# A macaron block in fp32 products: transposes of both layers moved from TensorE to transposing DMAs of 16-bit halves

## The reference

```
x = x + 0.5 * ffn(layernorm(x))
x = x + attn(layernorm(x))
x = x + 0.5 * ffn(layernorm(x))

ffn(x):  shared = silu(x @ Ws_up) @ Ws_down
         aff = x @ centroids.T;  top 8 of 64 experts by aff + bias
         w = sigmoid(aff of the chosen) / their sum
         routed = sum over the chosen experts of w_e * (silu(x @ W_up[e]) @ W_down[e])
attn(u): xf = u[:1], then u[1:] @ WB.T;  xb = u[1:] @ WBf.T, then u[-1:]
         gamma = sigmoid(xf @ w1 + xb @ w2 + b);  y = gamma * (xf + xb) + (1 - gamma) * u
```

## Time and profile before

| | |
|---|---|
| median of 3 runs | 790.46 us (790.07 to 790.76) |
| the profiled execution, its own time | 790.69 us |
| its span, first to last instruction | 788.5 us |
| PE busy | 777.0 us (99%) |
| DVE busy | 656.8 us (83%) |
| ACT busy | 634.4 us (80%) |
| POOL busy | 436.6 us (55%) |
| granted clock of TensorE | full (2.4 GHz) over all the span |

### The profile page before, as it was taken

The page is one execution under the profiler, slowest core; times in us unless marked ns, Lnnn a source line. Parts: engine busy times, 40 slices in busy tenths (PEclk is TensorE's granted clock), DMA queues, the critical chain, the costliest instruction groups (busy, mean ns, idle before and its releaser), DMA issues.

```text
span 788.5 us, 12421 instructions
## 1 busy us (share of the span) xinstructions
PE 777.0 (99%) x3621; PEld 641.4 (81%) x3621; DVE 656.8 (83%) x1423; ACT 634.4 (80%) x1221; POOL 436.6 (55%) x404
## 2 busy tenths in 40 slices
PE   7999999999999999999999999999999999999998
PEld 6777878888888888888888888888888888888786
DVE  6787989879898798977989789897898888788875
ACT  7987778888878888778887779787788887886885
POOL 4785646565555554645646456464554645554453
PEclk9999999999999999999999999999999999999999
DMA  8000000100000000100001000010000000000000
GB/s 287 15 1 14 1 1 1 27 16 16 11 8 21 27 13 0 27 0 27 13 0 27 0 27 13 0 27 0 27 13 0 13 1 27 13 1 1 13 1 14
DMA packets 26973, 14.66 MB, mean 19 GB/s; under 512 B 13248, under 2 KB 25792, under 8 KB 26944
## 3 DMA queue, kind: packets, MB, share of 16 engines
q1 hardware_dynamic: 26944, 14.30, 6.2%
HBM read 9.05 MB, written 2.10 MB: 14 GB/s over the span
## 4 chain that ended last, share of the span: by engine, by line
PE 86%; DVE 6%; ACT 5%; issue 2%; POOL 1%; ACTq 0%; DVEq 0%
PE up L855 13%; PE up L857 13%; PE up L856 13%; PE y_ps L855 13%; PE y_ps L857 13%; PE y_ps L856 13%; PE side L864 2%; ACT g_hi L520 2%; ACT up L486 2%; PE side L873 2%; DVE gated L709 1%; DVE g_lo L718 1%; PE side L906 1%; PE side L905 1%; POOL g_lo L373 1%
## 5 line engine op out<-in xcount | busy, mean ns | idle before, releaser
L373 POOL TENSOR_TENSOR g_lo<-gated,g_hi 128x512 fp32r<-128x512 f32 x256 | 331.6, 1296 | 309.9 <-ACT g_hi L520 309.4
L486 ACT ACTIVATE up<-up 128x512 f32<-128x512 f32 x513 | 302.2, 589 | 63.5 <-PE up L857 62.4
L709 DVE TENSOR_TENSOR gated<-up,cw 128x512 f32<-128x512 f32 x256 | 175.6, 686 | 73.0 <-ACT up L486 68.4
L855 PE MATMUL y_ps<-g_hi,wd_hi 128*128 128x512 f32 x512 | 204.3, 399 | 1.3 <-POOL g_lo L373 1.2
L855 PE MATMUL up<-x_hi,wu_hi 128*128 128x512 f32 x512 | 200.5, 392 | 1.0 <-DVE g_lo L718 1.0
L857 PE MATMUL y_ps<-g_hi,wd_lo 128*128 128x512 f32 x512 | 199.9, 390 | 0.0
L857 PE MATMUL up<-x_hi,wu_lo 128*128 128x512 f32 x512 | 199.6, 390 | 0.0
L856 PE MATMUL y_ps<-g_lo,wd_hi 128*128 128x512 f32 x512 | 199.5, 390 | 0.0
L856 PE MATMUL up<-x_lo,wu_hi 128*128 128x512 f32 x512 | 199.3, 389 | 0.0
L709 DVE TENSOR_TENSOR up<-up,cw 128x512 f32<-128x512 f32 x256 | 177.0, 691 | 19.7 <-ACT up L486 17.7
L520 ACT CAST g_hi<-up 128x512 fp32r<-128x512 f32 x256 | 151.6, 592 | 46.2 <-DVE up L709 43.7
(11 more groups left out here) (128 smaller groups left out, 518.1 us busy)
## 6 DMA issues: line engine op xcount, KB each, us to landing
x_in<-in_x SPq DMA_DIRECT2D x8, 256.0 KB, 2.7
wu_raw<-in_w_up SPq DMA_DIRECT2D x4, 512.0 KB, 7.9
wd_raw<-in_w_down SPq DMA_DIRECT2D x4, 512.0 KB, 8.6
x_res<-in_x SPq DMA_DIRECT2D x8, 256.0 KB, 2.8
out<-out_sb SPq DMA_DIRECT2D x7, 256.0 KB, 2.2
mix<-in_mix SPq DMA_DIRECT2D x1, 389.0 KB, 7.3
out<-out_sb SPq DMA_DIRECT2D x2, 128.0 KB, 1.9
cw_halves<-w_halves SPq DMA_TRANSPOSE x12, 2.7
```

The source lines that it names most:

```text
L373: nc.gpsimd.tensor_tensor(g_lo[:, i, :], gated[:, t // 2 % ORING, :], g_hi[:, i, :].bitcast(fp32), ALU.subtract).then_inc(lo_done[1], 1)
L486: nc.scalar.activation(up[i][:, :], up[i][:, :], ACT.Silu).then_inc(silu_done, 1)
L709: nc.vector.tensor_tensor(gated[:, t // 2 % ORING, :] if t % 2 else up[i][:, :], up[i][:, :], cw[ph.q][:, :], ALU.mult).then_inc(gate_done, 1)
L855: nc.tensor.matmul(o, a[0], b[0], start=start, stop=False)
```

## The change

In phases 3 to 13 no transposes on PE are left. Each of the five paths (weights, x of the first layer, x of the third layer, u, y) goes this way: the fp32 values are taken as pairs of 16-bit words; POOL copies the first words of all values side by side, then the second words (two packs, `pack`); SP issues one transposing DMA for the 128 x 1024 words; POOL writes the turned halves back into their places (two joins, `join_...`). For y, ACT's copy out of PSUM packs itself, by writing the two kinds of words apart. The weights' join moves from ACT to POOL. The copies on ACT of x and of u go. In phase 2 the new x of the first layer goes by DMA too, with its packs in phase 1, and phase 2 packs the x of the third layer for phase 3. `x1` and `last_sum` read the joined y in SBUF. SP's order becomes, in the loop: x of the third layer, y, load of x, store, load of the residual, weights, x of the first layer, y, u, weights.

The tables move steps to other slots (before and after):

```
 AT_THIRD = {
-    "x_t": 4, "x_copy": 4, "x_split": 5, ... "cw_pack": (15, 17), "cw_copy": 23,
+    "x_join": (1, 3), "x_split": 5, ... "cw_pack": (17, 21), "cw_join": (25, 27),
...
-    "stat2": (29, 30), "aggr2": 30, "rstd2": 31, "norm2": (33, 34),
+    "stat2": (29, 30), "aggr2": 30, "rstd2": 31, "norm2": (33, 34), "x2_pack": (33, 34),
 AT_STEADY_A = {
-    "x_t": 6, "x_copy": 6, "x_split": 9, "aff": 10, "sig": 13, "bias": 11, "max": 13, "take": 13,
-    "gate": 13, "sum": 13, "inv": 21, "cw_pack": (21, 23), "cw_copy": 29,
-    "y_t": 6,
-    "stat0": (20, 22), "aggr0": 24, "rstd0": 25, "norm0": (28, 30),
-    "y": 2, "out": 8, "keep": 11,
+    "x2_join": (1, 3), "x_split": 15, "aff": 9, "sig": 13, "bias": 11, "max": 13, "take": 13,
+    "gate": 13, "sum": 13, "inv": 21, "cw_pack": (21, 23), "cw_join": (29, 31),
+    "y_join": (5, 7), "out": 10, "keep": 13, "y": 2,
+    "stat0": (16, 17), "aggr0": 18, "rstd0": 19, "norm0": (22, 24), "x_pack": (25, 27), "x_join": (33, 34),
 AT_STEADY_B = {
-    "x_t": 1, "x_copy": 1, "x_split": 3, "aff": 6, "sig": 8, "bias": 7, "max": 8, "take": 8,
-    "gate": 8, "sum": 8, "inv": 15, "cw_pack": (15, 17), "cw_copy": 23,
-    "y_t": 6, "x1": 8, "stat1": (10, 12), "aggr1": 13, "rstd1": 14, "norm1": (16, 18), "xu": 19, "u_t": 22,
-    "u_copy": 22, "attn": 25, ...
+    "x_split": 9, "aff": 5, "sig": 8, "bias": 7, "max": 11, "take": 11,
+    "gate": 12, "sum": 12, "inv": 15, "cw_pack": (25, 26), "cw_join": (29, 30),
+    "y_join": (5, 7), "x1": 7, "stat1": (8, 9), "aggr1": 10, "rstd1": 10, "norm1": (13, 14), "xu": 23, "u_pack": (15, 17), "u_join": (19, 21),
+    "attn": 25, ... "norm2": (33, 34), "x2_pack": (33, 34),
```

The new steps:

```
+            def turn(halves, turned, done):
+                rows_in = halves.rearrange("p h n c -> p (h n c)") if len(halves.shape) == 4 else halves.rearrange("p h t -> p (h t)")
+                sp.dma_start(turned[:, :, :, :].rearrange("p h n c -> p (h n) c"), rows_in, transpose=True).then_inc(done, 16)
...
+            def pack(halves, h, made, words_of, value, done):
+                if h == 0:
+                    hold(pool, made, value)
+                last = nc.gpsimd.tensor_copy(halves[:, h, :, :], words_of)
+                if h == 1:
+                    last.then_inc(done, 1)
...
+            def join_x(q, h, moved, value, splits):
+                if h == 0:
+                    hold(pool, x_lo_done[1 - q], splits)
+                    hold(pool, moved, value)
+                made = nc.gpsimd.tensor_copy(words(x_raw[:, :], h), plane(n_turned_halves, h))
...
+            def join_u(c, h):
...
+                made = nc.gpsimd.tensor_copy(words(u_mid[:, 1:T], h), plane(n_turned_halves, h)[:, 1:T])
...
+            def join_y(ph, h):
+                dst = out_sb if ph.post is not None else x1
...
+                made = nc.gpsimd.tensor_copy(blocks_of(dst[:, :, :], h), y_turned_halves[:, h, :, :])
...
-            def cw_join(ph):
-                act.wait_ge(cw_moved, 16 * (ph.p - 1))
-                nc.scalar.copy(halves_of(cw[1 - ph.q][:, :], NB), cw_halves[:, :, :, :]).then_inc(cw_done[1 - ph.q], 1)
...
+                if by_dma:
+                    planes = y_ps[:, :].bitcast(u16).rearrange("p (t h) -> p h t", h=2)
+                    nc.scalar.copy(y_halves, planes).then_inc(y_copied, 1)
...
-                        nc.vector.scalar_tensor_tensor(x1[:, :, :], side_rows[0], 0.5, x_res[:, :, :],
+                        nc.vector.scalar_tensor_tensor(x1[:, :, :], x1[:, :, :] if ph.y_dma else side_rows[0], 0.5, x_res[:, :, :],
```

More of the change, by code:

```diff
@@ L51, in __init__ @@
         self.late_act = at.get("late_act", self.late)
-        self.cw_dma = prep is not None and "cw_pack" in at
+        self.cw_dma, self.x_dma = "cw_pack" in at, prep is not None and "x_t" not in at
+        self.y_dma, self.u_dma = "y_join" in at, "u_join" in at
         self.use = p // 2 if isinstance(p, int) else use
@@ L380, in pack_weights @@
-                halves = w_norm[:, :, :].bitcast(u16).rearrange("p n (e h) -> p n e h", h=2)[:, :, :, h]
-                made = nc.gpsimd.tensor_copy(w_halves[:, :, h, :].rearrange("p n (e r) -> p n e r", r=R),
-                                             halves.unsqueeze(3).to_broadcast([P, NB, E, R]))
+                if h == 0:
+                    hold(pool, dup_done[1 - ph.q], n + 1 - (ph.q == 1))
+                made = nc.gpsimd.tensor_copy(w_halves[:, h, :, :].rearrange("p n (e r) -> p n e r", r=R),
+                                             blocks_of(w_norm[:, :, :], h).unsqueeze(3).to_broadcast([P, NB, E, R]))
@@ L383, in pack_weights, with join_weights @@
                 if h == 1:
                     made.then_inc(w_packed, 1)
+            def join_weights(ph, h):
+                q = 1 - ph.q
+                if h == 0:
+                    hold(pool, cw_moved, 16 * (ph.p - 1))
+                made = nc.gpsimd.tensor_copy(words(cw[q][:, :], h), plane(cw_turned_halves, h))
+                if h == 1:
+                    made.then_inc(cw_done[q], 1)
+            def join_x(q, h, moved, value, splits):
+                if h == 0:
+                    hold(pool, x_lo_done[1 - q], splits)
+                    hold(pool, moved, value)
+                made = nc.gpsimd.tensor_copy(words(x_raw[:, :], h), plane(n_turned_halves, h))
+                if h == 1:
+                    made.then_inc(x_copied[q], 1)
@@ L425, in phase @@
                         pack_weights(ph, ph.at["cw_pack"].index(t))
+                    if t in ph.at.get("cw_join", ()):
+                        join_weights(ph, ph.at["cw_join"].index(t))
+                    if t in ph.at.get("x_pack", ()):
+                        h = ph.at["x_pack"].index(t)
+                        pack(n_halves, h, norm_done[0], blocks_of(normed[0][:, :, :], h), ph.norm0 + 1, x_packed)
+                    if t in ph.at.get("x_join", ()):
+                        c = ph.norm0 if ph.norm0 is not None else ph.prep[2]
+                        join_x(1, ph.at["x_join"].index(t), x_moved, 16 * (c - 1), c)
+                    if t in ph.at.get("x2_join", ()):
+                        join_x(0, ph.at["x2_join"].index(t), x2_moved, 16 * ph.prep[2], ph.prep[0])
+                    if t in ph.at.get("x2_pack", ()):
+                        h = ph.at["x2_pack"].index(t)
+                        pack(n_halves, h, norm_done[2], blocks_of(normed[2][:, :, :], h), ph.mid + 1, x2_packed)
+                    if t in ph.at.get("u_pack", ()):
+                        h = ph.at["u_pack"].index(t)
+                        pack(n_halves, h, norm_done[1], blocks_of(normed[1][:, :, :], h), ph.mid + 1, u_packed)
+                    if t in ph.at.get("u_join", ()):
+                        join_u(ph.mid, ph.at["u_join"].index(t))
+                    if t in ph.at.get("y_join", ()):
+                        join_y(ph, ph.at["y_join"].index(t))
                     if ph.at.get("xu") == t:
@@ L570, in phase @@
                     if ph.at.get("cw_copy") == t:
[L571 to L574, removed]
+                        cw_copy(1 - ph.q, ph.prep[0])
                     if ph.at.get("u_copy") == t:
@@ L989, in phase @@
                     if ph.at.get("y_t") == t:
[L990 to L993, removed]
+                        pe.wait_ge(cw_done[ph.q], ph.use + 1)
                         turn_y(ph.p)
```

82 lines of the change are left out of this document (60 added, 22 removed).

## The result

The changed kernel takes 792.00 us (median of 20 runs, 791.25 to 793.26) against 790.48 us before (20 runs, 790.07 to 791.27). The ratio is 1.0019, with a 95% interval of 1.0013 to 1.0026. The forecast was 785.4 us, faster; 792.00 lies within its range of 779 to 794 us, but on the other side of the kernel before. The transposes left PE as forecast and nothing was gained: the time that they took came back as waits of PE.

What follows compares the result with a forecast made beforehand. PE, busy 99% of the span, was taken as the bound: 790.69 - 12.6 (transposes) - 1.95 (waits ending odd phases) + 7.8 (waits starting odd phases) + 1.5 (even phases) = 785.4 us, range 779 to 794 us.

Steps and rivals of the forecast that it cites:

- three groups of 0.45 us: Even phases 4 to 12: transposes of x, y and u leave PE, each group of four worth 0.45 us.
- a wait of 0.3 us at T0+25: Middle of five even phases: DVE's low part 14 late by 0.3 us, 1.5 us in all, bounds 0 and 2.0.
- The wait at the end of odd phases: End of phases 3, 5, 7, 9, 11: PE's wait for DVE's g_lo goes, 5 times 0.39, 1.95 us.
- the chain at the start is hidden: Rival, odd phase start: packs, DMA and join 1.3 us shorter, no PE wait, 777.6 us; chance 0.15 with cases between.
- The last sum of an odd phase is turned in the same way, but DVE has two slots of room there.: Odd phases: last sum also gets both inputs in SBUF and can wait for POOL; no cost counted.
- So PE waits 1.3 us, in all six odd phases.: Odd phase start: x2's packs, DMA and half join delay POOL's low part 1 to T0+8.2; 7.8 us back.
- The wait for y: Odd phases, product that clears y_ps, due T0+5.90: up to 0.4 us for ACT's copy, inside the 1.3 us wait.
- the same collision with joins of 0.61 us: Rival, even phases: x1 behind POOL's low part 7 though joins take 0.61 us; 791.9 us, chance 0.14.
- the 0.7 us named as the limit: Rival "x1 behind POOL", even phases: joins above about 0.7 us make x1 1.3 us late; 795.4 us, chance 0.26.

Runs made afterwards that it cites:

- second experiment: Changed kernel with the last sum of odd phases at DVE's slot 9 instead of 10; 790.25 us, ratio 1.0001 to the kernel before.
- first experiment: Changed kernel with the x2 join of odd phases at POOL's slots 3 and 5, not 1 and 3, behind low part 1; 785.47 us, ratio 0.9934.

## Why the prediction was wrong

**What held.** PE lost 112 transposes. An even phase was to lose three groups of 0.45 us and gain a wait of 0.3 us at T0+25, 1.05 us in all; it lost three groups, gained 0.31 us and is 1.1 us shorter. (The restart of 0.11 us behind this wait had no price, but the same restart behind the wait at the end of odd phases went.) The wait at the end of odd phases went (0.39 us in each of five). The wait for POOL's low part 1 came, in all six odd phases, at T0+7 and later, by the very chain that was laid out: packs, 2.7 us of DMA, half a join, low part. The rival "the chain at the start is hidden" was made true by moving the join two slots, and the kernel then took 780.81 us with the last sum moved too, where that rival had 777.6. The forecast had seen no way to shorten the wait; it looked for an earlier norm, and not for a later join.

**What failed.** The sum had -5.25 us in the profiled span, where +0.6 was measured. The 5.9 us between them are, by term:

- *"The last sum of an odd phase is turned in the same way, but DVE has two slots of room there."* This is the step that failed by its reasoning. The form, the collision and the place were seen, and its price was set to nothing from room that was not worked out. The last sum took 1.80 us in each odd phase, DVE caught up only 0.7 of the 1.1 us, and PE waited 0.26 + 0.11 us ten microseconds on: 6 x 0.38 = 2.3 us, which the odd phases of the second experiment get back.
- *"So PE waits 1.3 us, in all six odd phases."* The mechanism was right and the size was off, by 2.6 us, the largest of the terms. In phases 7, 9 and 11 PE stops for 0.25 us (y's copy) and for 1.30 + 0.11 us (low part 1), 1.66 us together. The wait for y does lie inside, as the forecast had it: low part 1 comes at a fixed time, whatever PE waited for ahead of it. What was short is the chain. It ended at T0+8.54 for 8.2: the packs 0.15 us later, and DMA with its signals 3.0 us for 2.8. From the join's start to the low part's pass 0.70 us, the step from 6.2 to 6.9 that the forecast had. And the restart of 0.11 us, noted as slow, had no price. With phase 13 (1.55 us), phase 3 (1.35 us) and phase 5 the term is 10.4 us for 7.8.
- *Phase 5* holds 0.8 us of that: the late landing of the weights ahead of it.
- *Terms that were not in the sum:* phase 1, 0.6 us, which go with the packs moved into it, a phase at which the forecast did not look; in phase 2 a group of 0.45 us returned only 0.08, since a product behind it now waits 0.44 us for POOL's low part, where 0.13 us were lost before; hundredths in the odd phases, 0.3 us.

These are 2.3 + 2.6 + 0.6 + 0.4 + 0.3 = 6.2 us, less 0.2 us by which the even phases did better, and roundings. Outside the span the changed kernel's profiled execution takes 2.7 us and that of before 2.2, another 0.5 us.

**The rivals.** The time that came is that of "the same collision with joins of 0.61 us" (791.9 us), but not for its reason: that the number fits is chance. x1 took 0.69 us in the changed kernel's profile, although the joins took longer than the 0.7 us named as the limit. The timelines of POOL and DVE in phase 6 (T0 = 304.78) show the margin:

```profile
315.74 0.77 POOL L462 COPY x<-y_turned_halves 128x512 uint16<-128x512 uint16 x1
316.85 1.63 POOL L410 TENSOR_TENSOR g_lo<-gated,g_hi 128x512 fp32r<-128x512 f32 x1 [0.34 <-ACT g_hi L617]
```
```profile
316.64 0.69 DVE L888 SCALAR_TENSOR_TENSOR x<-x,x_res 128x512 f32<-128x512 f32 x1
```

POOL idled 0.34 us behind the join, waiting for ACT, and x1 had begun at 316.64; so POOL's low part is the one that is held up, 1.63 us for 1.30. The limit was set wrong: by the forecast's own times (POOL free for the first join at 9.0, low part 7 possible at 12.0) two joins and a low part of 1.3 us have 3.0 us, which allows joins of 0.85 us. The mechanism itself is real and has its forecast size, as phase 4 of the first experiment shows, where y landed 1.5 us late.

The Trainium skill, SBUF — State Buffer, section SBUF: two separate sides, has the rule that stands behind most of this: a VectorE instruction with both inputs in SBUF and a GpSimd one that reads SBUF keep each other out for a whole instruction. This case agrees in both directions: 0.68 us became 1.80 for the last sum, 0.42 became 1.31 for w_norm, and POOL's 1.30 became 1.63 under x1.

## What to carry to other kernels

Moving work off the bounding engine pays only as much as its consumers' slack allows: here 12.6 us of transposes were removed, and two entries of a table decided whether the kernel was 0.2% slower or 1.2% faster. A step that waits for a DMA goes behind every instruction of its engine that does not need it. For an operation whose input moves from PSUM to SBUF, list what the other of VectorE and GpSimd does at that very moment; price a collision at up to the other's whole instruction, and carry it to the next due time before calling it room. Waits of one engine for two chains of fixed times don't add up, the later chain sets the sum; take the later one away and the earlier is still to pay.

## What the runs showed of the hardware

- POOL writes every second 16-bit word of 512 in 0.77 us, and reads every second one (a pack) in 0.61 us; ACT pays 1.38 for 1024 such writes and 1.00 for 1024 from PSUM written side by side.
- The waits of PE read here, from 0.11 us on, are each followed by one matmul that delays the next by 0.11 us (0.34 us from start to start for 0.23).
- A transposing DMA of 128 x 1024 words of 16 bits lands 2.7 us after its issue, but after 3.2 to 4.7 us where a fetch of instructions fell into it (38 of 383; not tested by taking the fetch away).
- A VectorE instruction with both inputs in SBUF that began 0.04 us behind a GpSimd low part took 1.80 us for 0.68; a slot earlier, with nothing on GpSimd, it took 0.68.
